# A bidirectional convolutional GRU over eight images, one NeuronCore: images innermost in the stores, the normalised image split ring by ring

## The reference, cut to what matters

```python
def step(h, xr):                       # one line of 32 cells of 8 images
    out = _gru_step(xi, h, wih, whh)   # r, z = sigmoid(.), n = tanh(i_n + r * h_n), (1 - z) * n + z * h
    ctx = out.reshape(b, L, c).transpose(0, 2, 1)
    h_new = jnp.tanh(_conv1d(ctx, cw, cb))
    return (h_new, ctx)
...
out = jnp.einsum('bchw,oc->bohw', context_map, w_comb) + b_comb[None, :, None, None]
...
x = x + _L0_conv_ref(_gn(x), ...)
```

## Time and profile before

| | us |
|---|---|
| median of 3 runs | 367.61 (366.99 to 367.64) |
| profiled execution, its own time | 366.35 |
| its span in the profile | 364.6 |
| TensorE / VectorE / ScalarE / GpSimd busy | 324.1 / 308.2 / 275.0 / 15.8 |

### The profile page before, as it was taken

The page is one execution under the profiler, slowest core; times in us unless marked ns, Lnnn a source line. Parts: engine busy times, 40 slices in busy tenths (PEclk is TensorE's granted clock), DMA queues, the critical chain, the costliest instruction groups (busy, mean ns, idle before and its releaser), DMA issues.

```text
span 364.6 us, 7973 instructions
## 1 busy us (share of the span) xinstructions
PE 324.1 (89%) x2702; PEld 261.3 (72%) x2702; DVE 308.2 (85%) x766; ACT 275.0 (75%) x573; POOL 15.8 (4%) x26
## 2 busy tenths in 40 slices
PE   0002798999999999999999999999999999999995
PEld 0002477888888888888888888888888888873442
DVE  0659989999998899999999999999899888987875
ACT  6538897888888888888888888888888888867400
POOL 1056101000000000000000000000000000000000
PEclk9999899999999999999999999999999999999999
DMA  7900000000000000000000000000000000000433
GB/s 301 375 0 1 1 2 0 2 0 0 0 0 0 0 0 0 0 0 0 0 0 0 0 0 0 0 0 0 0 0 0 0 0 0 0 0 36 174 138 115
DMA packets 4182, 10.43 MB, mean 29 GB/s; under 512 B 592, under 2 KB 720, under 8 KB 4176
## 3 DMA queue, kind: packets, MB, share of 16 engines
q1 hardware_dynamic: 4176, 10.36, 7.4%
HBM read 6.16 MB, written 4.19 MB: 28 GB/s over the span
## 4 chain that ended last, share of the span: by engine, by line
PE 85%; ACT 5%; DVE 4%; issue 2%; DMA 2%; POOL 1%; SPq 0%; ACTq 0%
PE rz_bank L690 22%; PE conv_bank L690 17%; PE rz_bank L693 11%; PE n_bank L690 11%; PE conv_bank L693 8%; PE n_bank L693 5%; DMA ctx_store<-weights_dram 2%; ACT ctx_store L342 1%; PE rz_bank L776 1%; PE n_bank L776 1%; PE rz_bank L780 1%; PE n_bank L780 1%; PE n_bank L778 1%; PE rz_bank L778 1%; DVE stats L489 1%
## 5 line engine op out<-in xcount | busy, mean ns | idle before, releaser
L690 PE MATMUL conv_bank<-ctx_store,w_parts 128*128 (+1 forms) x558 | 108.9, 275 | 1.4 <-ACT ctx_store L430 0.9
L690 PE MATMUL rz_bank<-h_parts,w_parts 128*128 128x256 f16 x372 | 76.2, 273 | 0.1
L407 ACT ACTIVATE rz<-rz_bank,descale 128x512 f32<-128x512 f32 x96 | 65.9, 686 | 7.9 <-PE rz_bank L690 2.4
L419 ACT ACTIVATE nval<-npre 128x256 f32<-128x256 f32 x93 | 38.4, 413 | 40.5 <-DVE npre L627 40.5
L693 PE MATMUL conv_bank<-ctx_store,w_parts 128*128 (+1 forms) x279 | 67.2, 275 | 0.0
L690 PEld LDWEIGHTS conv_bank<-ctx_store,w_parts 128*128 128x128 f16 x558 | 54.3, 98 | 17.2 <-ACT ctx_store L430 6.6
L615 DVE SCALAR_TENSOR_TENSOR npre<-n_bank,descale,rz 128x256 f32<-128x256 f32 x93 | 45.0, 484 | 24.5 <-ACT rz L407 24.3
L690 PE MATMUL rz_bank<-x_rows,w_parts 128*128 (+1 forms) x256 | 52.8, 274 | 2.0 <-issue 2.0
L424 ACT ACTIVATE hval<-conv_bank,biases,descale 128x256 f32<-128x256 f32 x93 | 52.0, 560 | 0.0
L693 PE MATMUL rz_bank<-h_parts,w_parts 128*128 128x256 f16 x186 | 45.7, 273 | 0.0
L690 PE MATMUL n_bank<-h_parts,w_parts 128*128 128x256 f16 x186 | 45.6, 273 | 0.0
(11 more groups left out here) (110 smaller groups left out, 499.6 us busy)
## 6 DMA issues: line engine op xcount, KB each, us to landing
x<-x_dram SPq DMA_DIRECT2D x8, 512.0 KB, 9.3
out_dram<-x_rows SPq DMA_DIRECT2D x16, 256.0 KB, 2.0
ctx_store<-weights_dram SPq DMA_DIRECT2D x3, 576.0 KB, 5.1
ctx_store<-weights_dram SPq DMA_DIRECT2D x1, 192.0 KB, 6.1
biases<-biases_dram SPq DMA_DIRECT2D x1, 2.0 KB, 11.6
```

The costliest lines, as they stand in the source:

```text
L407: nc.scalar.activation(rz[k][:].rearrange("p g c -> p (g c)"), rz_bank[k][:], ACT.Sigmoid, scale=gate_scale(k)).then_inc(sig_done[k], 1)
L690: last = nc.tensor.matmul(out, w_block(HI, k, n), parts(hi_or_lo), start=start, stop=stop and hi_or_lo == LO, skip_group_check=True)
```

## The change

Six things change together.

1. **Stores.** There is one context store [C, DIRS, STEPS, 2, PAD, B], with the images innermost, so each tap reads 256 adjacent elements, and a chunk of the output reads 512 columns of 2 rows of all images. The split image is [C, 2, H, W // 2, B, 2]: the two cells of a pair of columns are adjacent, and then come the images. A row is read with the images innermost, at a distance of two elements (4 bytes); a column likewise. x_col and its copy (L402) are gone, and so products of k = 2 read `x_rows` too.
2. **Rings.** The image is split into HI and LO by rings of two rows and two columns. The five pieces of the outer ring are split ahead of the loop and in block 0. Ring 1's six pieces go to blocks 3 to 6, and those of rings 2 to 7 go one to a block, blocks 7 to 40 (34 pieces). In such a block ScalarE's HI piece stands first, and VectorE's LO piece between `blend` and the wait for the gates. TensorE's input products of block n wait for all pieces of the blocks below n.
3. **Normalisation.** One batch of 8 images instead of three; edges first, then strips, the cores of the images in blocks 0 to 2. ScalarE takes the moments of images 1 and 4. The two weight sets not needed first are loaded after the images.
4. **Weights.** They are split in ten units of 384 columns. GpSimd scales the first six and takes their LO parts, ScalarE the HI parts; ScalarE and VectorE do the other four in blocks 0, 2, 3 and 12. The maximum over the partitions comes from two small products instead of GpSimd. GpSimd's power -1/2 stands behind its six units. TensorE runs 24 products into an unused bank in four groups ahead of the loop (`warm`; before 8 in one group).
5. **Loop.** Steps 0 to 14 are unrolled, the loop body holds two steps, since a column's place in its pair must be known.
6. **Output.** 16 chunks of 2 rows of all images; all three directions go to one bank, so there is one VectorE operation for each chunk, and 8 stores of 512 KB, whose pieces in memory are 512 bytes long (2048 before).

```diff
-        ctx_store = [sb(f"ctx_store_{k}", [C, 2, STEPS, B, PAD], f16) for k in range(DIRS)]
-        x_rows = sb("x_rows", [C, 2, H, B, W], f16)
-        x_col = sb("x_col", [C, 2, B, H], f16)
+        ctx_store = sb("ctx_store", [C, DIRS, STEPS, 2, PAD, B], f16)
+        x_rows = sb("x_rows", [C, 2, H, W // 2, B, 2], f16)
...
+def ring_pieces(i):
+    lo, hi, width = 2 * i, H - 1 - 2 * i, W - 2 * i
+    rows = [Cells((row, row + 1), (0, width)) for row in (lo, hi, lo + 1, hi - 1)]
+    if hi - lo < 4:
+        return rows
+    top, end = lo + 2, hi - 1
+    if i == 0:
+        return rows + [Cells((top, end), (width - 2, width))]
+    middle = (top + end) // 2
+    return rows + [Cells((top, middle), (width - 2, width)), Cells((middle, end), (width - 2, width))]
+RINGS = H // 4
+FIRST_RING = ring_pieces(0)
+def pieces_of_blocks():
+    pieces = ring_pieces(1)
+    found = {(1, 0): pieces[0:2], (1, 1): pieces[2:4], (1, 2): pieces[4:5], (2, 0): pieces[5:6]}
+    for i in range(2, RINGS):
+        first = DIRS * (2 * i - 2) + 1
+        for n, cells in enumerate(ring_pieces(i)):
+            found[divmod(first + n, DIRS)] = [cells]
+    return found
+SPLIT_IN_BLOCK = pieces_of_blocks()
+def splits_before(t, j):
+    return len(FIRST_RING) + sum(len(pieces) for block, pieces in SPLIT_IN_BLOCK.items() if block < (t, j))
...
+POOL_UNITS = ("in 0", "rec 0", "conv 0", "in 1", "rec 1", "conv 1")
+DVE_UNITS = ("in 2", "conv 2", "rec 2", "comb")
+UNITS = POOL_UNITS + DVE_UNITS
+UNITS_IN_BLOCK = {(0, 2): ("conv 2",), (1, 0): ("rec 2",), (4, 0): ("comb",)}
+CORE_ON_ACT = {(0, 1): (5,), (0, 2): (6, 7)}
+CORE_ON_DVE = {(0, 0): (0,), (0, 1): (1, 2), (0, 2): (3, 4)}
...
+            pool.wait_ge(scale_done, 1)
+            for unit in range(len(POOL_UNITS)):
+                n, lo, hi = unit_blocks(unit)
+                nc.gpsimd.tensor_tensor(out=merged(w32[:, lo:hi, :]), in0=merged(w32[:, lo:hi, :]),
+                                        in1=w_scale[:, n:n + 1].to_broadcast([C, GATES * C]), op=ALU.mult) \
+                    .then_inc(w_scaled, 1)
+                pool.wait_ge(w_scaled, unit + 1)
+                pool.wait_ge(w_hi_done, unit + 1)
+                nc.gpsimd.tensor_tensor(out=merged(w_parts[:, LO, lo:hi, :]), in0=merged(w32[:, lo:hi, :]),
+                                        in1=merged(w_parts[:, HI, lo:hi, :]), op=ALU.subtract) \
+                    .then_inc(w_lo_pool, 1)
+            pool.wait_ge(var_eps, 1)
+            nc.gpsimd.tensor_tensor(out=x_scale[:], in0=gvar[:], in1=minus_half[:], op=ALU.pow) \
+                .then_inc(pow_done, 1)
...
+            magnitude_sums(0)
+            magnitude_sums(1)
+            weights_hi(0)
+            image_moments(ACT_IMAGES[0])
+            for unit in range(1, 3):
+                weights_hi(unit)
+            image_moments(ACT_IMAGES[1])
+            for unit in range(3, len(POOL_UNITS)):
+                weights_hi(unit)
+            for k in (2, COMB):
+                magnitude_sums(k)
+            for b in ACT_NORMED:
+                normalise(b, edges)
+            for cells in FIRST_RING[0:2]:
+                x_hi(cells, 1)
+            for b in ACT_NORMED:
+                normalise(b, strip)
...
+            dve_normed = [b for b in range(B) if b not in ACT_NORMED]
             image_stats(0)
-            weight_scales()
...
+            sets_peak(0)
+            weight_scales(0)
+            for b in (2, 3, 5, 6, 7):
+                image_stats(b)
+            spread()
+            variance()
+            shift()
+            for b in dve_normed:
+                normalise(b, edges)
+            sets_peak(1)
+            for b in dve_normed[0:2]:
+                normalise(b, strip)
+            x_lo(FIRST_RING[0])
+            weight_scales(1)
+            x_lo(FIRST_RING[1])
+            for b in dve_normed[2:]:
+                normalise(b, strip)
+            for cells in FIRST_RING[2:4]:
+                x_lo(cells)
...
+                if isinstance(t, int):
+                    if (t, j) == (0, 0):
+                        context_lo(*now)
+                        weights_lo(UNITS.index("in 2"))
+                        for cells in FIRST_RING[4:]:
+                            x_lo(cells)
+                    for unit in UNITS_IN_BLOCK.get((t, j), ()):
+                        weights_lo(UNITS.index(unit))
+                    for b in CORE_ON_DVE.get((t, j), ()):
+                        normalise(b, core)
+                    for cells in SPLIT_IN_BLOCK.get((t, j), ()):
+                        x_lo(cells)
                 if exists(nxt[1]) and not is_first(nxt[1]):
                     reset_hidden(*nxt)
...
                 def x_parts(part):
-                    store = x_col if k == 2 else x_rows[:, :, line(k, s), :, :]
-                    return store[:, part, :, :].rearrange("p b l -> p (b l)")
+                    if k == 2:
+                        pair, one = column_cells(s)
+                        return x_rows[:, part, :, pair, :, one]
+                    return x_rows[:, part, line(k, s), :, :, :].rearrange("p v b w -> p v w b")
...
+                if isinstance(t, int) and 0 < t < UNROLLED:
+                    pe.wait_ge(x_lo_done, splits_before(t, j))
+                if is_first(s) and k == 1:
+                    pe.wait_ge(x_lo_done, 2)
+                elif is_first(s) and k == 2:
+                    pe.wait_ge(x_lo_done, len(FIRST_RING))
...
+            for c in range(CHUNKS):
                 dve.wait_ge(y_ready, c + 1)
                 dve.wait_ge(x_biased, c + 1)
...
+                part = c % STORE_CHUNKS
                 nc.vector.scalar_tensor_tensor(
...
+                    y_sb[:, c // STORE_CHUNKS, :, part * CHUNK_ROWS * W:(part + 1) * CHUNK_ROWS * W],
+                    y_bank[c % RING][:].rearrange("p (s b) -> p b s", b=B),
+                    descale[:, COMB_SET:COMB_SET + 1], residual(c), ALU.mult, ALU.add).then_inc(y_summed, 1)
```

More of the change, by code:

```diff
@@ L81, in build @@
         hval = [sb(f"hval_{k}", [C, COLS], f32) for k in range(DIRS)]
-        context = [sb(f"context_{k}", [C, B, PAD], f32) for k in range(DIRS)]
+        context = [sb(f"context_{k}", [C, PAD, B], f32) for k in range(DIRS)]
         h_parts = [sb(f"h_parts_{k}", [C, 2, COLS], f16) for k in range(DIRS)]
@@ L173, in build @@
         y_ready = sem("y_ready")
-        y_rows_summed = sem("y_rows_summed")
         x_biased = sem("x_biased")
@@ L192, in is_first, with column_cells @@
             return isinstance(step, int) and step == 0
+        pair_column = [None]
+        def column_cells(s):
+            if isinstance(s, int):
+                return divmod(line(2, s), 2)
+            return pair_column[0]
         def blocks(eng, block):
-            for t in (0, 1):
+            for t in range(UNROLLED):
                 for j in range(DIRS):
                     block(t, j)
-            with eng.Fori(2, STEPS - 1) as t:
-                for j in range(DIRS):
-                    block(t, j)
+            with eng.Fori(0, PAIRED) as i:
+                for part in range(2):
+                    pair_column[0] = i * -1 + PAIRED - part, part
+                    for j in range(DIRS):
+                        block(i * 2 + (UNROLLED + part), j)
+            pair_column[0] = None
             for t in (STEPS - 1, STEPS):
@@ L330, in _, with moment, magnitude_sums @@
             nc.scalar.activation(first_sigmoid[:], minus_half[:, 0:1], ACT.Sigmoid)
-            for k in range(DIRS + 1):
+            moments = [0]
+            def moment(instruction):
+                moments[0] += 1
+                instruction.then_inc(act_moments, 1)
+                act.wait_ge(act_moments, moments[0])
+            def magnitude_sums(k):
                 act.wait_ge(w_loaded[k], 16)
@@ new lines, in warm @@
+            def warm(products):
+                for _ in range(products):
+                    nc.tensor.matmul(rz_bank[2][:], w_block(HI, 0, 0),
+                                     merged(w_parts[:, HI, DIRS:DIRS + OUT_COLS // C, :]),
+                                     start=True, stop=True, skip_group_check=True)
+            pe.wait_ge(pool_built, 6)
+            turn_sums(0)
+            spread_peaks(0)
+            pe.wait_ge(w_hi_done, 2)
+            warm(FRONT_WARM)
+            pe.wait_ge(aggr_done, B - len(ACT_IMAGES))
@@ L721, in input_products @@
                     pe.wait_ge(npre_done[k], s - 1)
-                passes(n_bank[k][:, 0:COLS], k, 2, x_parts, HI, start=True)
-                last = passes(n_bank[k][:, 0:COLS], k, 2, x_parts, LO, stop=first)
+                passes(lines(n_bank[k][:, 0:COLS]), k, 2, x_parts, HI, start=True)
+                last = passes(lines(n_bank[k][:, 0:COLS]), k, 2, x_parts, LO, stop=first)
                 if first:
```

529 lines of the change are left out of this document (251 added, 278 removed).

## The result

| | before | after |
|---|---|---|
| median, us | 367.30 (4 runs) | 379.94 (378.54 to 380.50, 4 runs) |
| profiled execution, its own time | 366.35 | 380.04 |
| its span | 364.6 | 377.6 |

The ratio is 1.0343, 95% interval 1.0307 to 1.0379: slower by 3.4%, where 1.1% was forecast (371.5). The time lies inside the range (360 to 381), at its upper end; the rise is about three times the forecast one. The span rose by 13.0 instead of 4.0.

What follows compares the result with a forecast made beforehand. TensorE was taken to bound the loop. Start -1.2, ring stretch +9.7, other blocks -2.4, output products -2.3, VectorE operation -0.8, store +1.0 summed to +4.0: span 368.6, median about 371.5 us, range 360 to 381.

Steps and rivals of the forecast that it cites:

- The input products' reading ... I take nothing.: Input products reading rows and columns at 4-byte steps: no added cost taken, bounded above by 109 ns more per product.
- its forecast: Blocks 41 to 94: shorter convolutions and no column copy gap, 0.045 us a block over 53 blocks, -2.4 us.
- the strided rival: Input products from block 7 on: strided reads double 109 to 218 ns, time 446 us; chance 0.15.
- 34 x 0.286 = +9.7: Blocks 7 to 40: input products wait for VectorE's late LO piece, 3.275 us a block against 2.99, +9.7 us.
- three units 1.6: Start, blocks 0 to 3: VectorE's three weight units give back 1.6 us of the 8.7 us lead.
- Net -1.2: Start to block 7: first input product 8.7 us earlier, 7.5 given back by VectorE's remaining work, net -1.2 us.
- run beside these: Start: ScalarE's three image cores, 1.0 us each, run in parallel with VectorE's remaining work.
- The bound of +4: Start: upper bound of +4 us if ScalarE's work is in series with VectorE's and the clock is low longer.
- the end: From block 94's convolution: cheaper output products, one VectorE operation fewer and a dearer last store, -2.1 us.
- The store: Last output store of 512 KB in 512-byte pieces: landing +0.6 to +3 us longer, +1.0 taken.
- The rival on the faster side: Blocks 8 to 41: LO pieces seen by 156.83, no wait, 360.3 us; or more start lead survives; together chance 0.25.
- "pieces cost more" case: Ring stretch and store: long end of their terms, TensorE's waits lower its clock for part, 376 to 381 us; chance 0.15.

Runs made afterwards that it cites:

- the last but one kernel: Kernel after with earlier pieces, older waits, output weights in block 42, start reordered, rows as even then odd cells: 362.07 us, ratio 0.9833 to the kernel before.
- the group with steps of 16 bytes: Eight products with unused results, read at steps of 16 bytes, run behind the last chunk in a kernel of added reads: 451 ns a product.

## Why the prediction was wrong

The direction and its main mechanism were right, and the sum was short by 9.0 us of span. By its steps:

1. **"The input products' reading ... I take nothing."** This step failed, and it is the largest part. A row product takes 120 ns, not 109. In each block that reads a row that is 0.09 to 0.10 us, two blocks of three: blocks are 3.04, 3.04 and 2.95 instead of 2.945 throughout, some 3.5 us from block 41 on, of the 4.1 by which that stretch missed its forecast. With rows read at 113 ns that stretch fell from 160.1 to 158.1 us. With no pairs and 109 ns it took 157.4, with other waits in it. I asked only what a step of 4 bytes costs, and for that nothing was nearly right (110 for a column, and 113). The row has a second property, a new run after every eighth element, and the trace of before had already priced odd run starts, in a figure of this same prediction (the 0.02 by which a convolution is longer). It was used to weigh the strided rival and never multiplied by the new number of runs: 16 odd ones at 0.8 ns are 13 ns, close to the 11 measured. The closeness is in part luck, since 32 runs from odd elements in the column order cost nothing.
2. **"34 x 0.286 = +9.7".** The wait and the cycle were right: between blocks 14 and 41 a block takes (177.02 - 88.21) / 27 = 3.289, and 3.275 was worked out. (The number is a little better than its parts: the row products' 0.1 in some inputs is in the 3.289 and was not in the 3.275.) Missing is the unit in block 12, 1.7. The prediction put "three units 1.6" into the start and named none for the ring stretch, though the change lists block 12. The rest of the 2.4 is 0.4 from the 27 blocks' excess over 3.275 and 0.3 in the blocks ahead of block 12. Block 41's own inputs still wait for the last piece, 0.4, which is counted in the next stretch.
3. **"Net -1.2" at the start.** First input product at 31.55 (32.7 forecast), but 11.0 given back instead of 7.5. VectorE's work was counted. Two things were not: that this work stands as a whole in front of pieces that TensorE waits for, and ScalarE's cores, said to "run beside these", in front of a context (stands of 2.97, 2.02 and 2.20 us); and that TensorE then runs at 1.2 GHz for longer (6.5 us of longer products, where the kernel before had 1.7). With the power and ScalarE's cores moved block 4 came 3.0 us earlier, but how the 2.3 us missed here are shared among the stands and the clock no run separates. The bound of +4 held it.
4. The other terms held: convolution 0.98, chunks 1.94 (1.96 forecast), the end -1.9 (-2.1, in which the products' term adds up to 2.2 by its own figures and not 2.3). GpSimd took 0.82 and 0.91 instead of 0.94 twice. The store lands in 3.2 us instead of 2.0, +1.2 for +1.0. The span stands 2.4 below the execution's own time instead of 1.75.

The rival of strided reading at twice the price did not come: a step of 4 bytes takes 113 ns, and twice the price is reached only at 8 bytes (227). The rival on the faster side did not come either, but its point of decision was well placed: with the piece in time, the ring stretch takes 104.1 and in the last but one kernel 102.1 (101.6 before), and with that kernel's other edits the change is a gain. The "pieces cost more" case had the time in its band (376 to 381) by luck: the pieces cost 384 ns for 224 elements, as worked out, and the clock in the ring stretch was 1.00.

## What to carry to other kernels

In this loop a wait placed one block after its producer cost what the producer was late, over and over (11.1 us of stands in 34 blocks): let the consumer wait for what it reads, and give the producer a block more. When a layout changes, price every operand's whole pattern, its step, the length of its runs and where each run begins, for the engine that reads it and the ones that write it. Work with a far due time has no place ahead of work that a neighbour waits for.

## What the runs showed of the hardware

- TensorE reads 2-byte elements at nearly full pace at steps of 4 bytes (113 ns for 256, adjacent 109), but steps of 6 bytes take 180 and of 8 bytes 227 at the same granted clock, 1.00. The Trainium skill ("Advanced Engine Details and Errata", section on memory cachelines) asks for at least two hits on a 16-byte line. That two are enough, as the prediction took it, is not borne out here: 8 bytes make two hits and cost double.
- A bank can be written in runs of 8 float32 with gaps at no cost (109), while single elements at steps of 32 bytes cost double (215 and 216 in the kernel that wrote its rows so).
- A ring piece whose 2-byte elements lie 16 bytes apart takes some 4.8 ns an element on VectorE ((1215 - 446) / 160 between pieces of 224 and 64), which also reads the HI part so, and 5.0 on ScalarE, which only writes so. In pairs of adjacent elements, the pairs 32 bytes apart, the same pieces take 1.0 and 0.9.
- The granted clock can fall although TensorE is never idle. In the group with steps of 16 bytes, behind that with 8, and in the two groups after it:

```profile
388.97:392.59 3.62, 3.62 (x10) 0.95 (x9) 0.00 (x0) 0.00 (x0) 0.00 (x0) 0.84 0.00 0
392.59:399.70 7.11, 7.11 (x17) 2.00 (x16) 0.00 (x0) 0.00 (x0) 0.00 (x0) 0.50 0.00 0
```

TensorE is busy for all of it, at 430 to 460 ns a product, and its clock goes to 0.84 and 0.50. By the last products of the run, which follow at 216 ns, it was back. Ahead of the fall stood only products that read slowly (227, then 451 ns). Whether that made the clock fall no run tried apart, and the kernel ran once.
